# GpSimd prefills the bias buffers with the mask term and adds the bias by accumulating transfers

## The chip, the cores and the metric

The kernel runs on 1 core of one Trainium2 chip. The metric is the device time of one execution in microseconds, as the median of the runs.

## The reference

The model has four layers on 8 samples of 512 tokens with 256 features. The change touches the first, an attention block with 16 heads of 16 features, and the small inputs (token ids and angles) from which conditions are worked out. What matters of it:

```python
emb = silu(sin_emb(timestep)) @ W_ada + b_ada
scale, shift = split(emb[:, None, :], 2)
x = ln(src) * (1.0 + scale) + shift
q, k, v = heads(x @ Wq + bq), heads(x @ Wk + bk), heads(x @ Wv + bv)
scores = einsum('bhqd,bhkd->bhqk', q / sqrt(HEAD_DIM), k)
scores = scores + attention_bias          # (8, 16, 512, 512) float32, 134 MB
scores = where(src_mask, -inf, scores)    # (8, 1, 512, 512) bool
ctx = einsum('bhqk,bhkd->bhqd', softmax(scores), v)
x = x + (ctx @ Wo + bo)
# then a feed-forward layer, an adapter chosen by token, a rotation by angles, a second adapter
```

## The kernel before, in words

`attention_block` computes the first layer's attention, `network_block` behind it everything else, sample by sample. The change is in the first, in `setup_programs` (conditions), in `load_layouts`, and in the host part that lays out the small inputs.

Attention goes sample by sample: the first and the last are written out, the six between are a loop on each engine. A sample has STEPS = 64 steps, one for each head (16) and tile of 128 queries (4). Step n on TensorE (`iteration` in the tensor program): `scores` for step n + 3 (one bf16 matmul with 512 columns, L539, of stacked pieces of q and k, and one with the identity that adds the mask term, L540), four steps out of 16 `weigh` (values times turned probabilities, L562), `turn` (four 128x128 transposes of the probabilities, L549), and what `SPARE` places on two spare banks: transposes of x, projections Q, K, V of the next sample, context and output projection. VectorE adds the bias and takes the minimum of the negated row in one instruction (`add_bias`, L679, two steps ahead) and copies 3 of 8 turned tiles (L688); ScalarE takes the exponent (L820, one step ahead) and copies the other 5 of 8 (L827). So every engine has an order written out by hand, and semaphores with counts per sample stand between them.

The bias lies in `bias` (the buffer `big`): NB = 4 buffers of [128, 4, 512] float32, one per head. SP's program runs by heads: at head h of a sample it waits until VectorE has added the bias of all 4 tiles of head h (`biased`), then loads head h + 4 into the same buffer (`load_bias`, L415, 1 MB, its source rows of 2 KB). In the same queue, behind these waits, stand at fixed heads the loads of x, mask, the expert's weights, the stores of the pieces (`store_pieces`, L442, three transfers for q and three for k in each half of the heads), the loads of the stacks (`load_stack`, L453) and the store of x1.

The mask arrives as bytes in `mraw`. GpSimd makes from it the term (mask x -1e30, bf16) in two copies: `mterm_early` for heads 0 to 13 (L950, at step 56 for the next sample) and `mterm_late` for heads 14 and 15 (L958, at step 12), in four parts of 512 elements each. GpSimd also has, in this order within a sample: `copy_values` (L939, steps 5, 39, 41, 56), `keep_residual` (L967, step 15) and the four `cut`s (L925 to L929) at CUT_STEPS = 25, 26, 28, 31, in which the projections become three bf16 pieces. Cuts 2 and 3 wait until the stores of the pieces of cuts 0 and 1 have landed.

Ahead of the first sample `setup["load"]` issues ten loads on SP (token ids, angles four times, frequencies, pairs, W_ada, b_ada), then `first_loads` (x, identity, Wq, Wk, bq, bk, mask, Wv, bv, Wo, bo, and the bias of heads 0 to 3). VectorE waits for all ten before it works out the angles (L149 on), and four cuts of the first sample are made on VectorE, in the order of the banks, the value projection last.

## Time and profile before

| | us |
|---|---|
| median of 3 runs | 1149.35 |
| lowest and highest | 1147.81, 1149.48 |
| the profiled execution's own time | 1147.64 |
| its span, first to last instruction | 1145.8 |
| TensorE busy in the span | 1026.5 (90%) |
| VectorE busy | 818.1 (71%) |
| ScalarE busy | 776.6 (68%) |
| GpSimd busy | 349.4 (30%) |
| DMA, moved in all | 230.23 MB |

The page gives the busy time of each engine, the span in 40 slices of 28.6 us, the chain that ended last, the groups of instructions by line, and the transfers. PE is TensorE's matmul, PEld its weight load, DVE is VectorE, ACT ScalarE, POOL GpSimd, SP the engine that issues the transfers (SPq is its queue). L540 is line 540 of the kernel. Averages over the span hide that the first two thirds (attention) and the last third (network) have different limits; each stretch must be read by itself. "Idle before" names what a group waited for.

### The profile page before, as it was taken

What the parts mean: (1) busy time and instruction counts of PE and PEld (TensorE: products, weight loads), DVE (VectorE), ACT (ScalarE), POOL (GpSimd) and SP (SyncE); (2) the same over time, 40 slices, a digit from 0 to 9 for tenths busy, and PEclk for the clock granted to TensorE, in tenths of its full rate; (3) what the DMA queues carried; (4) which work ended last, traced back from release to release, by engine and by line L of the source; (5) the groups of instructions that cost most, each with busy time, mean ns of one, the idle gap of its engine ahead of it and who ended that gap; (6) DMA issues with size and microseconds to landing.
All of it is one profiled execution on the core that took longest, in us unless ns stands there. A gap on an engine that the chain in (4) does not pass through costs nothing. (4 is left out here: it accounts for less than half of the span.)

```text
span 1145.8 us, 21120 instructions
## 1 busy us (share of the span) xinstructions
PE 1026.5 (90%) x6128; PEld 670.0 (58%) x6128; DVE 818.1 (71%) x2056; ACT 776.6 (68%) x1238; POOL 349.4 (30%) x464
## 2 busy tenths in 40 slices
PE   2599999999999999999999999983999989898862
PEld 2456556656656565655655665642777767676641
DVE  5586775876787777778678686764456978897665
ACT  2287877887787788778788787863457565765442
POOL 0205114213312322320511511004455555654421
PEclk9799999999999999999999999996999999999976
DMA  7787976986995995896796797641111110101001
GB/s 237 241 299 262 353 274 232 367 294 225 338 326 191 340 349 204 305 356 233 275 362 245 250 371 266 247 151 37 38 37 38 37 55 18 55 18 37 19 19 37
DMA packets 131288, 230.23 MB, mean 201 GB/s; under 512 B 8992, under 2 KB 58016, under 8 KB 127136
## 3 DMA queue, kind: packets, MB, share of 16 engines
q1 hardware_dynamic: 131232, 229.59, 56.8%
q8 instruction: 22, 0.36, 0.1%
q14 instruction: 34, 0.28, 0.1%
HBM read 187.62 MB, written 41.94 MB: 200 GB/s over the span
## 5 line engine op out<-in xcount | busy, mean ns | idle before, releaser
L679 DVE CUSTOM_DVE_ANT_0 prob<-s_bank,big 128x512 f32<-128x512 f32 x512 | 344.8, 686 | 128.7 <-PE s_bank L540 103.0
L820 ACT ACTIVATE prob<-prob,nmax 128x512 f32<-128x512 f32 x512 | 359.6, 722 | 36.4 <-DVE nmax L679 35.2
L549 PEld LDWEIGHTS t_bank<-ident,prob 128*128 128x128 f32 x2048 | 241.0, 141 | 196.7 <-issue 71.2
L549 PE MATMUL t_bank<-ident,prob 128*128 128x128 f32 x2048 | 316.0, 277 | 8.0 <-DVE pt L688 4.7
L827 ACT COPY pt<-t_bank 128x512 f32<-128x512 f32 x320 | 185.1, 578 | 98.6 <-PE t_bank L549 98.0
L539 PE MATMUL s_bank<-stack_k,stack_q 128*128 128x512 bf16 x512 | 195.6, 382 | 4.6 <-DVE nmax L679 2.6
L540 PE MATMUL s_bank<-mterm_early,ident_bf 128*128 128x512 bf16 x448 | 170.8, 381 | 0.0
L688 DVE COPY pt<-t_bank 128x512 f32<-128x512 f32 x192 | 132.0, 687 | 48.9 <-PE t_bank L549 48.9
L562 PE MATMUL o_bank<-pt,val 128*32 128x512 f32 x1024 | 135.8, 604 | 0.7 <-ACT pt L827 0.7
L1624 POOL TENSOR_TENSOR gl<-big,gh 128x512 fp32r<-128x512 f32 x64 | 87.1, 1372 | 86.3 <-DVE gh L1329 86.3
L939 POOL TENSOR_SCALAR val<-vst 128x64 f32<-128x64 f32 x128 | 27.0, 245 | 251.8 <-PE o_bank L562 217.9
L1511 ACT ACTIVATE big<-bank,b 128x512 f32<-128x512 f32 x64 | 43.5, 689 | 42.8 <-PE bank L1191 41.9
L925 POOL TENSOR_SCALAR pieces<-proj 128x512 bf16<-128x512 f32 x28 | 17.4, 620 | 174.9 <-ACT proj L857 122.9
L539 PEld LDWEIGHTS s_bank<-stack_k,stack_q 128*128 128x128 bf16 x512 | 50.0, 98 | 26.6 <-issue 14.0
L1191 PE MATMUL bank<-hh,w1h 128*128 128x512 f32 x128 | 54.4, 425 | 11.6 <-ACT big L1511 6.7
L1210 PE MATMUL bank<-gh,w2h 128*128 128x512 f32 x128 | 54.0, 422 | 0.0
L562 PEld LDWEIGHTS o_bank<-pt,val 128*32 128x32 f32 x1024 | 20.4, 108 | 55.3 <-issue 51.8
L1191 PE MATMUL bank<-hh,w1l 128*128 128x512 f32 x128 | 51.7, 404 | 0.0
L1191 PE MATMUL bank<-hl,w1h 128*128 128x512 f32 x128 | 51.6, 403 | 0.0
L540 PEld LDWEIGHTS s_bank<-mterm_early,ident_bf 128*128 128x128 bf16 x448 | 44.2, 99 | 11.7 <-issue 7.8
L1210 PE MATMUL bank<-gh,w2l 128*128 128x512 f32 x128 | 50.9, 398 | 0.0
L1336 DVE TENSOR_TENSOR x24l<-x,x24h 128x512 fp32r<-128x512 f32 x32 | 47.9, 1536 | 1.0 <-ACT x24h L1519 0.5
(176 smaller groups left out, 1620.1 us busy)
## 6 DMA issues: line engine op xcount, KB each, us to landing
big<-in_fside_Bx16xSxS SPq DMA_DIRECT2D x128, 1024.0 KB, 6.6
pieces_dram<-pieces SPq DMA_DIRECT2D x64, 384.0 KB, 7.8
stack_q<-pieces_dram SPq DMA_DIRECT2D x16, 1024.0 KB, 8.0
stack_k<-pieces_dram SPq DMA_DIRECT2D x16, 1024.0 KB, 8.7
pieces_dram<-pieces SPq DMA_DIRECT2D x32, 256.0 KB, 7.5
xin<-in_x SPq DMA_DIRECT2D x8, 512.0 KB, 6.6
x_dram<-x SPq DMA_DIRECT2D x8, 512.0 KB, 2.6
big<-x_dram SPq DMA_DIRECT2D x8, 512.0 KB, 3.5
```

Source lines behind the costliest of these rows:

```text
L539: pe.matmul(bank, stack_q[:, h, t * P:(t + 1) * P], stack_k[:, h, :], start=True, stop=False)
L540: pe.matmul(bank, ident_bf[:], mterm[:, t, :], start=False, stop=True).then_inc(scored.sem, 1)
L549: last = pe.transpose(t_bank[n % 2][:, c * P:(c + 1) * P], prob[:, n % NT, c * P:(c + 1) * P], ident[:])
L562: last = pe.matmul(o_bank[VW * j:VW * (j + 1), :], val[:, c, G * g + j, :], pt[:, pt_slot(G * g + j), c, :], start=(c == 0), stop=(c == QT ...
L679: dve.tensor_tensor_reduce(out=prob[:, n % NT, :], in0=s_bank[n % 3][:, :], in1=bias[:, h % NB, t, :], scale=-1.0, scalar=3e38, op0=ALU.ad ...
L688: dve.tensor_copy(pt[:, pt_slot(h), :, t * P:(t + 1) * P], t_bank[n % 2][:, :].rearrange("p (c q) -> p c q", c=QT)).then_inc(evac[1].sem, 1)
L820: act.activation(tile, tile, ACT.Exp, bias=nmax[:, n % NT:n % NT + 1], scale=-1.0).then_inc(exped.sem, 1)
L827: act.copy(pt[:, pt_slot(h), :, t * P:(t + 1) * P], t_bank[n % 2][:, :].rearrange("p (c q) -> p c q", c=QT)).then_inc(evac[0].sem, 1)
L1191: last = pe.matmul(bank[f % 2][:, :], w[:, c, col], h[:, c, :], start=(n == 0), stop=(n == len(parts) - 1))
L1210: last = pe.matmul(bank[c][:, :], w[:, f, c * P:(c + 1) * P], gx[:, f, :], start=(m == 0), stop=(m == len(parts) - 1))
L1336: dve.tensor_tensor(x24l[:, l, c], src[:, c], x24h[:, l, c], ALU.subtract).then_inc(low_done[l].sem, 1)
L1624: pool.tensor_tensor(gl[:, f], g[:, f % NGT], gh[:, f], ALU.subtract).then_inc(gl_done.sem, 1)
```

## The change

The mask term is added no longer by TensorE. GpSimd writes it in float32 into a bias buffer as soon as that buffer is free, and then itself issues the load of the bias with accumulation (`accum_op=ADD`), so that the buffer ends up with bias plus mask term. TensorE's second matmul of each step, the bf16 identity and one of the two copies of the term go. The bias loads leave SP's program, with their waits. The mask term is made in one instruction of 2048 elements at step 49. GpSimd issues a load at the end of each head's last step (steps 3, 7, 11, ... in its order), between its cuts and value copies.

On the host, token ids are laid out in one array and angles, frequencies, pairs and the vectors b_ada, bq, bk, bo in another, so that two loads take the place of twelve; W_ada is loaded behind x. In the first sample the value projection is moved on VectorE between the cuts.

```diff
-    conds = [
-        (tok[:], d["itok_B_34_63"].partition_broadcast(P)), (dom[:], d["itok_B_0_15"].partition_broadcast(P)),
-        (arg[:, 2], d["condB_theta"].partition_broadcast(P)), (arg[:, 3], d["condB_theta"].partition_broadcast(P)),
-        (arg[:, 4], d["condB_phi"].partition_broadcast(P)), (arg[:, 5], d["condB_phi"].partition_broadcast(P)),
-        (freq[:], d["freq"]), (pairs[:], d["pairs"]), (w_ada, v["W_ada"]), (b_ada[:], v["b_ada"]),
-    ]
+        sp.dma_start(toks[:], d["toks"]).then_inc(vecs_in, 16)
+        sp.dma_start(vecs[:], d["vecs"]).then_inc(vecs_in, 16)
+
+    def load_weights(sp):
+        sp.dma_start(w_ada, v["W_ada"]).then_inc(w_ada_in, 16)
...
-EARLY_TERM_AT = QT * EARLY_HEADS
-LATE_TERM_AT = 12
+TERM_AT = 49
...
-        early = [(k["ident"][:], d["ident"]), (w["wq"], v["Wq"]), (w["wk"], v["Wk"]), (vec["bq"][:], v["bq"]),
-                 (vec["bk"][:], v["bk"])]
-        later = [(w["wv"], v["Wv"]), (bv[:], d["L0_cond_bv"].partition_broadcast(P)), (w["wo"], v["Wo"]),
-                 (vec["bo"][:], v["bo"])]
+        early = [(k["ident"][:], d["ident"]), (w["wq"], v["Wq"]), (w["wk"], v["Wk"])]
+        later = [(w["wv"], v["Wv"]), (bv[:], d["L0_cond_bv"].partition_broadcast(P)), (w["wo"], v["Wo"])]
...
-        first_loads += [(bias[:, h], v["bias"][:, h], bias_in[h]) for h in range(NB)]
...
-            for dst, src, arrived in first_loads:
+            for m, (dst, src, arrived) in enumerate(first_loads):
                 sp.dma_start(dst, src).then_inc(arrived, 16)
+                if m == 0:
+                    setup["load_weights"](sp)
...
-                    if not (last and h + NB >= H):
-
-                        sp.wait_ge(biased.sem, biased.at(b, QT * (h + 1)))
-                        apart(sp, sp_apart)
-                        load_bias(b, h + NB)
...
-                if n < QT:
-                    pe.wait_ge(early_term.sem, early_term.at(b - 1, n + 1))
-                if h == EARLY_HEADS:
-                    pe.wait_ge(late_term.sem, late_term.at(b, t + 1))
 
                 before = n - 3 if n >= 3 else (63, 61, 62)[n] - STEPS
                 pe.wait_ge(biased.sem, biased.at(b, before + 1))
                 bank = s_bank[n % 3][:, :]
-                mterm = mterm_early if h < EARLY_HEADS else mterm_late
-                pe.matmul(bank, stack_q[:, h, t * P:(t + 1) * P], stack_k[:, h, :], start=True, stop=False)
-                pe.matmul(bank, ident_bf[:], mterm[:, t, :], start=False, stop=True).then_inc(scored.sem, 1)
+                pe.matmul(bank, stack_q[:, h, t * P:(t + 1) * P], stack_k[:, h, :], start=True, stop=True
+                          ).then_inc(scored.sem, 1)
...
+            at = {use[:2]: m for m, use in enumerate(banks.uses)}
+            spare_use(banks, at["XT", 0], -1, first=True)
+            spare_use(banks, at["XT", 1], -1, first=True)
+            low_parts(-1)
+            dve.wait_ge(weights_in, 16 * len(later))
+            dve.wait_ge(w_high, 3)
+            dve.tensor_tensor(wl["wv"][:], w["wv"], wh["wv"][:], ALU.subtract).then_inc(w_low, 1)
+            cut(0)
+            cut(1)
+            spare_use(banks, at["V", 0], -1, first=True)
+            cut(2)
+            spare_use(banks, at["V", 1], -1, first=True)
+            cut(3)
...
-            def early_mask_term(b, t, first=False):
-                if t == 0:
-                    pool.wait_ge(mask_in.sem, mask_in.at(b, 16))
+            def mask_term(b):
+                pool.wait_ge(mask_in.sem, mask_in.at(b, 16))
+                apart(pool, pool_apart)
+                pool.tensor_scalar(mterm[:], mraw[:], MASKED, 0.0, ALU.mult, ALU.add).then_inc(term_done.sem, 1)
+
+            def load_bias(b, h, first=False):
+
+                if h % H == 0:
+                    pool.wait_ge(term_done.sem, term_done.at(b, 1))
                 if not first:
-                    pool.wait_ge(scored.sem, scored.at(b, QT * (EARLY_HEADS - 1) + t + 1))
+                    pool.wait_ge(biased.sem, biased.at(b, QT * (h - NB + 1)))
                 apart(pool, pool_apart)
-                pool.tensor_scalar(
-                    mterm_early[:, t, :], mraw[:, t, :], MASKED, 0.0, ALU.mult, ALU.add
-                ).then_inc(early_term.sem, 1)
-
-            def late_mask_term(b, t, first=False):
-                if t == 0 and not first:
-                    pool.wait_ge(scored.sem, scored.at(b - 1, STEPS))
+                pool.tensor_scalar(bias[:, h % NB], mterm[:], 1.0, 0.0, ALU.mult, ALU.add
+                                   ).then_inc(prefilled.sem, 1)
+                pool.wait_ge(prefilled.sem, h + 1 if first else prefilled.at(b, h - NB + 1))
                 apart(pool, pool_apart)
-                pool.tensor_scalar(
-                    mterm_late[:, t, :], mraw[:, t, :], MASKED, 0.0, ALU.mult, ALU.add
-                ).then_inc(late_term.sem, 1)
+                src = v["bias"][:, h] if first else v["bias"][:, bass.ds(b * H + h, 1)].rearrange(
+                    "p o t k -> p (o t) k")
+                pool.dma_start(bias[:, h % NB], src, accum_op=ALU.add).then_inc(bias_in[h % NB], 16)
 
             def keep_residual(b, first=False):
...
-                    if n == LATE_TERM_AT:
-                        for t in range(QT):
-                            late_mask_term(b, t, first=first)
-                    if not last and n == EARLY_TERM_AT:
-                        for t in range(QT):
-                            early_mask_term(b, t)
-
-            for t in range(QT):
-                early_mask_term(-1, t, first=True)
+                    if n % QT == QT - 1 and not (last and n // QT + NB >= H):
+                        load_bias(b, n // QT + NB)
+                    if not last and n == TERM_AT:
+                        mask_term(b)
+
+            mask_term(-1)
+            for h in range(NB):
+                load_bias(-1, h, first=True)
```

## Rows read from the trace of the kernel before

**Rows 1.** The page, the span in 40 slices: granted TensorE clock and DMA share, in tenths.
```profile
PEclk9799999999999999999999999996999999999976
DMA  7787976986995995896796797641111110101001
```

**Rows 2.** Table by stretches: stretch, length, busy us, clock, DMA share, GB/s.
```profile
50.00:762.00 712.00, 700.93 (x4664) 420.05 (x4664) 529.64 (x1432) 561.59 (x932) 172.44 (x308) 1.00 0.80 285
430.00:520.00 90.00, 88.86 (x598) 53.66 (x597) 66.71 (x179) 70.68 (x118) 23.66 (x41) 1.00 0.83 292
```

**Rows 3.** Groups by line, 430 to 520 us: busy, mean ns, idle before.
```profile
L679 DVE CUSTOM_DVE_ANT_0 prob<-s_bank,big 128x512 f32<-128x512 f32 x64 | 43.1, 685 | 16.5 <-PE s_bank L540 13.2 <-issue 3.1
L827 ACT COPY pt<-t_bank 128x512 f32<-128x512 f32 x40 | 23.1, 579 | 12.5 <-PE t_bank L549 12.4
```

**Rows 4.** Timeline of TensorE from 444 us: start, length, engine, line, operation.
```profile
444.52 0.38 PE L539 MATMUL s_bank<-stack_k,stack_q 128*128 128x512 bf16 x1
444.74 0.38 PE L540 MATMUL s_bank<-mterm_early,ident_bf 128*128 128x512 bf16 x1
445.05 1.06 PE L562 MATMUL o_bank<-pt,val 128*32 128x512 f32 x8
```

**Rows 5.** The page's issues of transfers: KB each, median us from issue to landing.
```profile
big<-in_fside_Bx16xSxS SPq DMA_DIRECT2D x128, 1024.0 KB, 6.6
pieces_dram<-pieces SPq DMA_DIRECT2D x64, 384.0 KB, 7.8
stack_q<-pieces_dram SPq DMA_DIRECT2D x16, 1024.0 KB, 8.0
```

**Rows 6.** Table by stretches, three short ones with the DMA engines full.
```profile
448.60:451.40 2.80, 2.80 (x18) 2.11 (x17) 2.05 (x7) 2.56 (x5) 0.00 (x0) 1.00 1.05 386
312.00:314.00 2.00, 2.00 (x17) 1.66 (x16) 1.96 (x8) 1.72 (x4) 1.81 (x3) 1.00 1.06 406
478.00:486.00 8.00, 8.00 (x61) 5.51 (x59) 7.73 (x24) 7.97 (x15) 0.00 (x0) 1.00 0.99 369
```

**Rows 7.** Line 415: issue ns min, median, max, first and last start; us to landing.
```profile
L415 SPq DMA_DIRECT2D big<-in_fside_Bx16xSxS x124: 367/373/1167, 55.5 to 745.6; - x124
...
DMA to landing us min/median/max: 5.0/6.5/14.4
```

**Rows 8.** Groups of GpSimd by line, whole span.
```profile
L950 POOL TENSOR_SCALAR mterm_early<-mraw 128x512 bf16<-128x512 uint8 x32 | 19.9, 621 | 17.9 <-DMA mraw<-in_mask_Bx1xSxS_bk 15.5
...
L967 POOL TENSOR_SCALAR xres<-xt 128x1024 f32<-128x1024 f32 x8 | 8.4, 1048 | 77.2 <-issue 77.2
```

**Rows 9.** Timeline of GpSimd around the cuts: first and last pieces of cuts.
```profile
452.59 0.62 POOL L925 TENSOR_SCALAR pieces<-proj 128x512 bf16<-128x512 f32 x1 [15.51 <-ACT proj L857]
...
455.36 1.17 POOL L929 TENSOR_TENSOR pieces<-rest,pieces 128x512 bf16<-128x512 f32 x1
...
459.58 1.17 POOL L929 TENSOR_TENSOR pieces<-rest,pieces 128x512 bf16<-128x512 f32 x1
...
467.25 0.62 POOL L925 TENSOR_SCALAR pieces<-proj 128x512 bf16<-128x512 f32 x1 [6.51 <-DMA pieces_dram<-pieces]
...
474.24 1.16 POOL L929 TENSOR_TENSOR pieces<-rest,pieces 128x512 bf16<-128x512 f32 x1
```

**Rows 10.** Timeline of SP in the same stretch.
```profile
459.35 4.90 SPq L442 DMA_DIRECT2D pieces_dram<-pieces  x6
```

**Rows 11.** Timeline of the start: SP, VectorE, TensorE.
```profile
0.73 0.40 SPq L130 DMA_DIRECT2D tok<-in_itok_B  x1
...
4.96 0.47 SPq L130 DMA_DIRECT2D b_ada<-in_L_cond_b_ada  x1
...
11.62 0.17 DVE L149 CAST tokf<-tok 128x8 f32<-128x8 int32 x1 [7.93 <-DMA b_ada<-in_L_cond_b_ada]
...
51.32 0.38 PE L539 MATMUL s_bank<-stack_k,stack_q 128*128 128x512 bf16 x1 [1.87 <-DVE vst L731]
```

**Rows 12.** Issues of transfers, two of the conditions: KB, us to landing.
```profile
tok<-in_itok_B SPq DMA_DIRECT2D x1, 4.0 KB, 2.2
...
b_ada<-in_L_cond_b_ada SPq DMA_DIRECT2D x1, 2.0 KB, 6.6
```

More of the change, by code:

```diff
@@ L90, in load_layouts @@
         v[w] = d["L0_cond_" + w].rearrange("(c p) n -> p c n", p=P)
-    for w in BY_FEATURE:
+    for w in BY_FEATURE[len(VECTORS):]:
         v[w] = d["L0_cond_" + w]
@@ L158, in angles @@
         link(dve.tensor_scalar(arg[:, 1], tokf[:, 1], freq[:, 0:1], None, ALU.mult))
-        link(dve.scalar_tensor_tensor(turns[:], arg[:], 1.0 / (2.0 * np.pi), quarter[:], ALU.mult, ALU.add))
+        link(dve.scalar_tensor_tensor(turns[:], arg, 1.0 / (2.0 * np.pi), quarter[:], ALU.mult, ALU.add))
         link(dve.tensor_scalar(turns[:], turns[:], 12582912.0, None, ALU.add))
@@ L164, in angles @@
         for part in TWO_PI_PARTS:
-            link(dve.scalar_tensor_tensor(arg[:], turns[:], -part, arg[:], ALU.mult, ALU.add))
-        link(dve.scalar_tensor_tensor(arg[:], quarter[:], 2.0 * np.pi, arg[:], ALU.mult, ALU.add))
-        dve.tensor_scalar(arg[:], arg[:], 3.1415925, -3.1415925, ALU.min, ALU.max).then_inc(sines, 1)
+            link(dve.scalar_tensor_tensor(arg, turns[:], -part, arg, ALU.mult, ALU.add))
+        link(dve.scalar_tensor_tensor(arg, quarter[:], 2.0 * np.pi, arg, ALU.mult, ALU.add))
+        dve.tensor_scalar(arg, arg, 3.1415925, -3.1415925, ALU.min, ALU.max).then_inc(sines, 1)
     def domains(dve):
-        link(dve.tensor_copy(k["domf"][:, 0], dom[:]))
+        link(dve.tensor_copy(k["domf"][:, 0], dom))
         link(dve.tensor_scalar(k["domf"][:, 1], k["domf"][:, 0], 0.0, E - 1.0, ALU.max, ALU.min))
@@ L193, in sines_of @@
         act.wait_ge(sines, 1)
[L194 removed]
+        act.activation(k["trig"][:], arg, ACT.Sin).then_inc(sines, 1)
         act.wait_ge(sines, 2)
@@ L793, in _ @@
                 dve.tensor_tensor(wl[name][:], w[name], wh[name][:], ALU.subtract).then_inc(w_low, 1)
[L794 to L806 removed]
+            dve.tensor_scalar(bq_scaled[:], vec["bq"], HD ** -0.5, None, ALU.mult).then_inc(bq_made, 1)
+            at = {use[:2]: m for m, use in enumerate(banks.uses)}
[11 more added lines that the diff above has]
+            cut(3)
             for n in range(2):
@@ L1751 @@
     place = np.arange(P) % 4
-    arrays["pairs"] = np.stack([place < 2, place >= 2], 1).astype(np.float32)
+    pairs = np.stack([place < 2, place >= 2], 1).astype(np.float32)
     beside = np.zeros((P, P), np.float32)
```

67 lines of the change are left out of this document (26 added, 41 removed).

## The prediction, made before the change was run

> **What bounds the kernel now.** I read the page's slices first. The kernel has two parts: attention over 8 samples, up to about 762 us, and the network behind it, which the change doesn't touch. In the first part TensorE is granted its full clock and the DMA share stands at 7 to 9 tenths; in the second the DMA share is one tenth [rows 1]. So only the first part can gain or lose much, and there two resources are near their end.
>
> The table by stretches gives both numbers. From 50 to 762 us TensorE is busy for 701 of 712 us at clock 1.00, ACT 562, DVE 530, GpSimd 172, and the DMA engines 0.80 of the time, which is 570 us. One sample in the middle (430 to 520) is the same: TensorE 88.9 of 90, DMA 0.83 [rows 2]. TensorE is the bound: DVE's bias line sits idle before PE's mask matmul, ACT's copy before PE's transposes [rows 3]. A sample takes 712 / 8 = 89 us, a step (one head, one tile of 128 queries, 64 steps per sample) 89.4 / 64 = 1.40 us. The second resource is what this change leans on: DMA has 142 us left in 712, and no more.
>
> **What the change takes from TensorE.** In the timeline of one step the score matmul starts at 444.52, the mask matmul at 444.74 and the next work at 445.05 [rows 4]. Starts 0.22 us apart are what a 512-column bf16 matmul takes of the pipeline; the 380 ns printed overlap. 512 such matmuls go: 512 x 0.22 = 113 us, all on the path that sets the end, if nothing else is late. The floor of the first part is then 712 - 113 = 599 us. ACT (562) and DVE (530) stay below that, with little room: they are the next two bounds.
>
> **What the bias transfers cost.** Per sample 16 bias loads of 1 MB, 12 stores of pieces and 4 stack loads [rows 5]. Short stretches at full share move 386 GB/s (448.6 to 451.4, a bias load alone at first) and 406 (312 to 314) [rows 6], so I take 400: 1.05 MB / 400 GB/s = 2.62 us of all 16 engines. The 124 loads issued in this part [rows 7] cost 124 x 2.62 = 325 of the 570 us; everything else 245. After the change each bias transfer must read the source, read what GpSimd wrote in SBUF, and write. No row of before shows such a transfer. The bounds: 1.0 times the plain load if the second read runs wholly beside the write, 2.0 times if the engine takes its reads one after another and they set its pace, as would a load and a store of the same 1 MB in a row. A count of passes (three for two) says 1.5. HBM is not what separates them, since it carries the same bytes. I take the middle between the count of passes and the count of reads, 1.75, because a stretch with loads and stores mixed (478 to 486) is already at share 0.99 with 369 GB/s [rows 6]: the engines, by their time per byte, are at their end, and there is no idle side into which a second read would fall. Demand: 570 + 0.75 x 325 = 814 us. At a share of 0.98 (the longest of these full stretches shows 0.99) that takes 831 us against 712 now: +119 us. With 1.5 it is (570 + 163) / 0.98 = 748, +36 us; with 2.0, 913, +201 us; with 1.0, 582, which is under TensorE's 599.
>
> The Trainium skill bears on this (Collectives: The Full Stack, "Part 3: Why 7x under link rate"): reduce-scatter runs at about half of all-gather's rate, 32.35 against 62.28 GB/s, since the add needs two reads on the same ring. By that ratio, 1.93, the first part would be at (570 + 0.93 x 325) / 0.98 = 890 us, +178; no run here shows an accumulating transfer yet. It speaks against the change, and it is the rival of the two reads below.
>
> **What GpSimd gets.** Its tensor_scalar takes 0.62 us for 512 elements and 1.05 us for 1024 [rows 8]: 0.84 ns per element and 0.19 us fixed, so 2048 elements take 1.9 us, if a bf16 source goes as the f32 and uint8 ones do; the ends are 1.7 (no fixed part) and 2.5 us (four times 0.62). Per sample: busy now 23.7; the two mask terms (8 x 0.62 = 5.0) become one of 1.9; 16 prefills add 30.4: 51 us. To this come 16 issues of a transfer. GpSimd issues none now; SP's take 0.37 us at the median and 1.17 at most [rows 7]. A queue that an engine has to fill itself may take longer than either; I take 1 us, with 0.4 and 3.5 as ends (the upper end an estimate: one issue per 1 MB at three times SP's slowest). 51 + 16 = 67 of 89 us: no bound by itself, and it becomes one at (89.4 - 51) / 16 = 2.4 us per issue.
>
> But GpSimd works in order. Queued ahead of a bias load are the four cuts of a sample and their waits. Cuts 0 and 1 run from 452.6 to 460.8, cut 2 waits until 467.25 for the store of the pieces, cut 3 ends at 475.4 [rows 9]. In the new order the load for head 10 (step 27) stands between cuts 1 and 2 and fits in that wait; the load for head 11 (step 31) stands behind cut 3. It would be issued at 475.4 + 1.9 + 1 = 478.3 and land 6.5 us later [rows 7], at 484.8. VectorE wants head 11 at its step 42, 17 steps after cut 0: 452.6 + 17 x 1.40 = 476.4. That is 8.4 us late. SP no longer waits for bias buffers ahead of the stores, which were issued at 459.35 though the first cut was done at 456.5 [rows 9, 10]: this gives 2.8 back. So 6 us of stall per sample (bounds 3 and 9), in the 7 samples that prepare the next: +42 us. Behind this wait stand all scores, so TensorE and ACT too. Before, the same load sat on SP, which nothing but the buffer held up. In a DMA-bound run this stall is also a time in which few bias loads are queued, so it adds up with the 119.
>
> **The start.** VectorE's first step on the conditions begins at 11.62, after the last of ten small loads, which was issued at 4.96; the first was issued at 0.73 [rows 11]. Two packed loads are issued by 1.6 and land 2.2 to 6.6 us later, as the small loads do [rows 12], so this start moves up by 3.4 to 7.8 us, take 6. The value projection now stands in the waits of the cuts; it is the last work ahead of the first scores at 51.32 [rows 11], but these also need the first stack loads, so 1 us. The loads of the first four heads start later and go through GpSimd; they have until the first scores and are done by about 33 us even at 3 us per issue. Sum -7 (bounds -10 and -2). The mask load, now released by one mask term, costs nothing: it is wanted some 50 steps after its issue.
>
> **Sum.** The profiled run of before has a span of 1145.8 and a time of 1147.6 us; the median of the runs is 1149.35, 1.7 above. 1147.6 - 7 + 119 + 42 = 1301.6, and 1.7 for the median: 1303 us. TensorE's 113 us vanish: its steps are 0.22 us shorter, and it waits for bias.
>
> **The rivals.**
> - Other side: the second read is free (factor 1.0). TensorE stays the bound at 599 us, DMA at 582 just under it: 1149.35 - 7 - 113 + 42 = 1071 us. For it: the read side of an engine may have room in a plain load, which the profile can't show since it prints one busy share for both sides. Against: the full stretches. Its place is the transfer from HBM to the bias buffer, its price 2.6 us. It decides as follows: with the stall of 42 and the start of -7 the first part may take 712 - 35 = 677 us, which is a demand of 663 = 570 + 93, so the factor must be below 1 + 93 / 325 = 1.29 for the kernel to be faster.
> - The two reads set the pace in full (factor 2.0): 1149.35 - 7 + 201 + 42 = 1385 us. For it: a load and a store of the same size in a row would cost that. Against: reads come from two memories, and the write of a plain load may be what fills its time.
> - GpSimd is the bound: if an issue takes 3 us, GpSimd has 51 + 48 = 99 us per sample and the 6.5 us that it waits for the store, 105.5. 8 x (105.5 - 89.4) = +129 us, 1149.35 - 7 + 129 = 1271 us. For it: it writes 2048 elements and describes 512 rows for each head. Against: only that it idles two thirds of its time now.
> - Nothing is gained or lost: factor near 1.29, 1149 us.
> - A part not doing what it says: if TensorE's time were not shortened since ACT is next, the fast case would lose up to 562 / 0.98 = 573 < 599, so nothing; I drop it.
>
> **Chances.** DMA-bound forecast 0.34, two reads in full 0.13, GpSimd-bound 0.17, fast 0.32, no change 0.04. The slower cases fall inside the range with the bounds of their costs: 1.5 with a stall of 3 per sample gives 1149 - 7 + 36 + 21 = 1199; 2.0 with 9 gives 1149 - 7 + 201 + 63 = 1406. The fast case begins at 1149 - 10 - 113 + 21 = 1047 if all goes well and sits at 1071. The likeliest case's own range is 1199 to 1370; the range for 8 in 10 reaches down to the fast case and up to two reads, 1065 to 1410. Faster by over 0.2% (about what a measurement of this kernel can tell from no change) 0.32, within 0.04, slower 0.64.
>
> **What would show it.** In the profile after: the DMA share in the first part at 9 to 10 tenths with less than 300 GB/s counted by bytes written, or, if it is GpSimd, its share near 9 tenths with DMA below 8. VectorE's bias line idle before the landing of bias transfers and not before TensorE. The time from issue to landing of a bias transfer at 9 us or more, against 6.6. Head 11 of each sample late by some us while GpSimd is in its cuts. VectorE's first step on conditions at 4 to 8 us. TensorE's busy share well below 0.9 and perhaps a clock below 1.00 as it waits. I am wrong if bias transfers land in 7 us or less with TensorE still busy for over 97% of a shorter first part.

## The result, and the profile after

The changed kernel takes 1276.16 us (median of 4 runs, 1275.11 to 1278.75) against 1148.58 for the kernel before beside it: 1.1117 times as long, 95% interval 1.1101 to 1.1134, or +128 us. The forecast was 1303, range 1065 to 1410, slower.

The profiled run of after has a span of 1273.1 us and a time of 1275.1. Its page, beside [rows 1]: the granted clock of TensorE and the share of the DMA engines in 40 slices, then the two queues (packets, MB, share of 16 engines), and the bias transfers (KB each, median us from issue to landing), which answer to [rows 5].

```profile
PEclk9798999789799989979988897899889999999966
DMA  7999999999999999999999999999201010100000
...
q0 software_dynamic: 67584, 134.23, 57.8%
q1 hardware_dynamic: 62208, 95.37, 21.9%
...
big<-in_fside_Bx16xSxS POOLq DMA_DIRECT2D x128, 1024.0 KB, 14.9
```

After the first slice (the start), every slice of the first part is at nine tenths or more, where before showed 5 to 9. In finer stretches of 10 us, from 60 to 880 us, after reads a share of 1.02 to 1.20; before is under 1.0 in 49 of its 69. The bias transfers stand in a queue of their own now (q0), and land 14.9 us after their issue at the median, 6.6 before. TensorE's granted clock is no longer full throughout.

The table by stretches (stretch, length, busy us of PE, PEld, DVE, ACT and POOL with counts, clock, DMA share, GB/s) answers to [rows 2]. The scores run in after from 53 to 891 us. In the 4 us of the second row nearly all that moves are accumulating transfers; in the 5 us of the third there are plain transfers beside them. They answer to [rows 6].

```profile
53.00:891.00 838.00, 670.92 (x4164) 396.27 (x4163) 524.88 (x1434) 562.40 (x935) 541.95 (x486) 0.91 1.11 243
526.00:530.00 4.00, 4.00 (x27) 3.12 (x26) 3.03 (x8) 3.85 (x8) 3.34 (x5) 1.00 1.12 206
530.00:535.00 5.00, 5.00 (x38) 3.35 (x37) 3.77 (x12) 3.84 (x7) 3.93 (x4) 1.00 1.09 336
```

The first part is 838 us long, 712 before: +126 of the +128. TensorE is busy for 671 of them, GpSimd for 542, and no engine is near its end but the DMA engines: share 1.11, at 243 GB/s where before had 285. The short stretch of accumulating transfers has 206 GB/s, half of the 386 and 406 of plain loads in [rows 6]: 1.049 MB / 206 GB/s = 5.1 us for a head's bias, 2.6 to 2.7 before. The 14.9 us from issue to landing hold waiting as well: one is issued every 838 / 124 = 6.8 us, so two or three are under way at a time, beside the plain ones.

Two groups of the page show who waits (busy, mean ns, idle before and its releaser); they answer to [rows 3] and [rows 8]. The two groups of issues behind them are of after and of the experiment e1 below, in which the same transfers are plain (issue ns min/median/max, first and last start).

```profile
L655 DVE CUSTOM_DVE_ANT_0 prob<-s_bank,big 128x512 f32<-128x512 f32 x512 | 339.1, 686 | 272.2 <-DMA big<-in_fside_Bx16xSxS 207.1
...
L933 POOL TENSOR_SCALAR big<-mterm 128x2048 f32<-128x2048 bf16 x128 | 259.2, 2025 | 76.1 <-DVE nmax L655 70.5
```

```profile
L939 POOL DMA_DIRECT2D big<-in_fside_Bx16xSxS x128: 1300/1307/1461, 15.6 to 874.7; - x128
...
DMA to landing us min/median/max: 8.9/14.9/22.4
```

```profile
L939 POOL DMA_DIRECT2D big<-in_fside_Bx16xSxS x128: 797/797/944, 14.6 to 759.0; - x128
...
DMA to landing us min/median/max: 5.5/6.0/12.5
```

VectorE's bias line stood 207 us before the landing of a bias transfer, where before it stood behind TensorE. GpSimd's write takes 2.0 us and its issue 1.3, 0.8 when the transfer doesn't accumulate.

The network behind attention is unchanged: from the last bias step to the end of the run lie 383.8 us (1275.1 - 891.3), before 383.6 (1147.6 - 764.0).

### The profile page after: what moved, and what is told of

Its sections match the earlier page's. It is cut to its first block and busy times, and to the rows that moved or that the text cites. A ratio compares the mean times of both kernels' runs of the same rounds, so it can differ in the third digit from the quotient of the medians.

```text
span 1273.1 us, 20268 instructions
## 1 busy us (share of the span) xinstructions
PE 993.3 (78%) x5616; PEld 642.1 (50%) x5616; DVE 822.4 (65%) x2055; ACT 775.7 (61%) x1238; POOL 737.2 (58%) x664
## 3 DMA queue, kind: packets, MB, share of 16 engines
q0 software_dynamic: 67584, 134.23, 57.8%
q1 hardware_dynamic: 62208, 95.37, 21.9%
## 5 line engine op out<-in xcount | busy, mean ns | idle before, releaser
L655 DVE CUSTOM_DVE_ANT_0 prob<-s_bank,big 128x512 f32<-128x512 f32 x512 | 339.1, 686 | 272.2 <-DMA big<-in_fside_Bx16xSxS 207.1
L526 PE MATMUL t_bank<-ident,prob 128*128 128x128 f32 x2048 | 352.2, 299 | 118.6 <-DVE pt L664 79.1
L526 PEld LDWEIGHTS t_bank<-ident,prob 128*128 128x128 f32 x2048 | 257.3, 152 | 316.8 <-DVE pt L664 111.7
L933 POOL TENSOR_SCALAR big<-mterm 128x2048 f32<-128x2048 bf16 x128 | 259.2, 2025 | 76.1 <-DVE nmax L655 70.5
L516 PE MATMUL s_bank<-stack_k,stack_q 128*128 128x512 bf16 x512 | 211.9, 415 | 61.3 <-DVE nmax L655 49.0
L939 POOL DMA_DIRECT2D big<-in_fside_Bx16xSxS x128 | 167.6, 1310 | 91.3 <-POOL big L933 85.6
L539 PE MATMUL o_bank<-pt,val 128*32 128x512 f32 x1024 | 142.5, 632 | 0.7 <-ACT pt L804 0.7
L516 PEld LDWEIGHTS s_bank<-stack_k,stack_q 128*128 128x128 bf16 x512 | 53.1, 104 | 90.6 <-DVE nmax L655 65.8
L916 POOL TENSOR_SCALAR val<-vst 128x64 f32<-128x64 f32 x128 | 39.4, 596 | 72.6 <-PE o_bank L539 54.8
L1372 DVE TENSOR_SCALAR xh<-bank,mv,rstd 128x256 f32<-128x256 f32 x96 | 45.6, 537 | 1.2
## 6 DMA issues: line engine op xcount, KB each, us to landing
big<-in_fside_Bx16xSxS POOLq DMA_DIRECT2D x128, 1024.0 KB, 14.9
```

The costliest lines, as they stand in the source:

```text
L516: pe.matmul(bank, stack_q[:, h, t * P:(t + 1) * P], stack_k[:, h, :], start=True, stop=True).then_inc(scored.sem, 1)
L526: last = pe.transpose(t_bank[n % 2][:, c * P:(c + 1) * P], prob[:, n % NT, c * P:(c + 1) * P], ident[:])
L539: last = pe.matmul(o_bank[VW * j:VW * (j + 1), :], val[:, c, G * g + j, :], pt[:, pt_slot(G * g + j), c, :], start=(c == 0), stop=(c == QT ...
L655: dve.tensor_tensor_reduce(out=prob[:, n % NT, :], in0=s_bank[n % 3][:, :], in1=bias[:, h % NB, t, :], scale=-1.0, scalar=3e38, op0=ALU.ad ...
L933: pool.tensor_scalar(bias[:, h % NB], mterm[:], 1.0, 0.0, ALU.mult, ALU.add).then_inc(prefilled.sem, 1)
L939: pool.dma_start(bias[:, h % NB], src, accum_op=ALU.add).then_inc(bias_in[h % NB], 16)
```

## The experiments

Twelve changed kernels follow. The kernel before took 1148.3 to 1148.6 us beside them. Some leave part of the mask out of the scores, as their texts say: they are there for their times.

| kernel | us | ratio (95%) |
|---|---|---|
| before | 1148.58 | |
| after | 1276.16 | 1.1117 (1.1101 to 1.1134) |
| e1 plain, GpSimd writes and issues | 1160.75 | 1.0105 (1.0088 to 1.0122) |
| e2 plain, SP issues, no write | 1084.89 | 0.9445 (0.9430 to 0.9461) |
| e3 the packed conditions alone | 1140.08 | 0.9921 (0.9904 to 0.9937) |
| e4 after, with a matmul of zeros per step | 1289.28 | 1.1211 (1.1182 to 1.1239) |
| e5 e1 with cuts 2 and 3 later | 1161.36 | 1.0121 (1.0104 to 1.0138) |
| e6 after with cuts 2 and 3 later | 1285.60 | 1.1192 (1.1171 to 1.1212) |
| e7 e3, accumulation for heads 4, 7, 9, 13 | 1183.45 | 1.0310 (1.0292 to 1.0327) |
| e9 e3, GpSimd adds in the buffer, 8 heads | 1138.51 | 0.9912 (0.9896 to 0.9929) |
| e10 e1 without GpSimd's write | 1148.97 | 1.0002 (0.9992 to 1.0011) |
| e11 after, accumulation in odd heads only | 1192.05 | 1.0381 (1.0363 to 1.0398) |
| e12 as e9, 6 heads | 1125.51 | 0.9805 (0.9788 to 0.9821) |
| e13 as e7, heads 4, 6, 8 | 1127.84 | 0.9825 (0.9809 to 0.9842) |

The theory: accumulating transfers fill the DMA engines and set the pace; behind it the loads that stand behind GpSimd's cuts. The rivals: GpSimd's work or its order alone does it, or TensorE's lower clock.

**e1, no accumulation.**

```
-                pool.dma_start(bias[:, h % NB], src, accum_op=ALU.add).then_inc(bias_in[h % NB], 16)
+                pool.dma_start(bias[:, h % NB], src).then_inc(bias_in[h % NB], 16)
```

> The changed kernel with the accumulation taken out of the transfer: GpSimd still writes the mask term into each buffer, still waits for it and still issues the load, but the load overwrites it. So the mask is left out of the scores. Theory A (the accumulating transfer takes the DMA engines twice as long, 5.1 us against 2.6 for 1 MB, and this sets the pace): the time falls from 1276 to 1040 to 1080 us, below the kernel before, and TensorE is busy for over 90% of the attention part. Theory B (GpSimd's 2 us of writing, 1.3 us of issuing and its order set the pace): it stays above 1200 us. Between 1040 and 1080 lies the stall behind the cuts that the prediction put at 42 us.

It takes 1160.75, between the ranges of the two theories, so neither forecast was met. Accumulation costs 1276.2 - 1160.8 = 115 us, and everything else together +12. So GpSimd as the bound falls as an account of the 128. But the rest isn't the gain that the prediction's fast case had: with each transfer at its plain price this kernel is still slower than before.

**e2, no work on GpSimd either.** The write is gone, and SP issues plain loads as before, behind its own waits; TensorE adds no mask.

```
+                    if not (last and h + NB >= H):
+                        sp.wait_ge(biased.sem, biased.at(b, QT * (h + 1)))
+                        load_bias(b, h + NB)
...
-                    if n % QT == QT - 1 and not (last and n // QT + NB >= H):
-                        load_bias(b, n // QT + NB)
```

> As e1_plain_pool, but GpSimd writes nothing into the buffers and SP issues the plain loads at the places they had before; the mask is left out of the scores. This is what taking the mask's matmul from TensorE is worth with nothing put in its place. Both theories: 1030 to 1045 us (1149 less 512 x 0.22 = 113, and some us of start). The difference to e1_plain_pool is what GpSimd's part costs by itself: 42 us by the prediction's stall behind the cuts, 5 or less if the four buffers cover it.

It takes 1084.89, some 40 us more than expected: TensorE's matmuls were worth less than 113 us. How much less, e3 tells.

**e3, the packed conditions alone**, on the kernel before: the two packed tensors, the late load of W_ada, the value projection between the cuts.

```
+        sp.dma_start(toks[:], d["toks"]).then_inc(vecs_in, 16)
+        sp.dma_start(vecs[:], d["vecs"]).then_inc(vecs_in, 16)
...
-        dve.wait_ge(cond_in, 16 * len(conds))
+        dve.wait_ge(vecs_in, 32)
```

> The kernel before with the packed conditions, the later W_ada and the value projection between the cuts, and nothing else of the change. If the start of the changed kernel is late since GpSimd's writes hold up VectorE there (its 128x2 operation took 2.78 us instead of 0.16), this kernel has its first scores 6 to 10 us earlier than before and takes 1139 to 1143 us. If the packing itself is worth nothing, since transfers of the pieces set the first scores, it stays within 2 us of 1149.

e3 takes 1140.08, 8 us less than before. From e3 to e2 the mask's matmuls go, with their waits, and GpSimd makes one mask term of 1.9 us in place of two (5.0 us a sample): 1140.1 - 1084.9 = 55 us, half of the 113 that the prediction took off TensorE's path. The same stretch of both, e3 first:

```profile
60.00:690.00 630.00, 618.52 (x4074) 374.26 (x4151) 465.88 (x1253) 494.62 (x820) 164.69 (x286) 1.00 0.82 287
```

```profile
60.00:690.00 630.00, 593.02 (x3959) 348.18 (x4033) 499.06 (x1362) 530.56 (x895) 144.36 (x238) 1.00 0.87 311
```

The groups of VectorE's bias line in these stretches count the steps:

```profile
L677 DVE CUSTOM_DVE_ANT_0 prob<-s_bank,big 128x512 f32<-128x512 f32 x442 | 298.2, 686 | 116.2 <-PE s_bank L538 94.3 <-issue 20.6
```

```profile
L668 DVE CUSTOM_DVE_ANT_0 prob<-s_bank,big 128x512 f32<-128x512 f32 x486 | 321.5, 685 | 79.6 <-PE s_bank L529 46.4 <-remote 20.4 <-issue 11.5
```

A step is 630 / 442 = 1.425 us in e3 and 630 / 486 = 1.296 in e2. TensorE's busy time per step goes from 618.5 / 442 = 1.399 to 593.0 / 486 = 1.220, 0.18 less, near the 0.22 of the prediction; its idle time grows from 0.026 to 0.076. Of 0.22 us a step, 0.13 arrived: over 512 steps 66 us, of which the run shows 55. In the busiest stretches the next engines are full, as in this one of e2, where VectorE is busy for 14.73 of 15 us and ACT for 14.29:

```profile
385.00:400.00 15.00, 13.62 (x78) 7.80 (x77) 14.73 (x45) 14.29 (x24) 1.05 (x1) 1.00 0.84 320
```

That these take the idle 0.05 fits, but what each idle piece waits for was not separated.

**e10, GpSimd issues but doesn't write.** e1 without these lines:

```
-                pool.tensor_scalar(bias[:, h % NB], mterm[:], 1.0, 0.0, ALU.mult, ALU.add
-                                   ).then_inc(prefilled.sem, 1)
-                pool.wait_ge(prefilled.sem, h + 1 if first else prefilled.at(b, h - NB + 1))
```

> e1_plain_pool without GpSimd's write into the buffer and the wait for it: GpSimd only issues the plain loads, in the same order among its cuts and copies; the mask is left out of the scores. e5 showed that moving two cuts is worth nothing, so the 76 us between e2 (1085) and e1 (1161) are open. If they come from what GpSimd has to do per head (1.9 us of writing and 0.7 of waiting, which make its loads late after each pile-up), this kernel is at 1085 to 1100 us. If they come from GpSimd issuing (its queue, the order behind the cuts), it stays at 1140 to 1160.

It takes 1148.97, 64 us more than e2, from which it differs in who issues the loads and in what order. The queue itself isn't slow: its loads land 7.9 us after their issue at the median, 7.4 in e2. Its timeline of GpSimd, and VectorE's step behind it (start, length, engine, line, operation, idle before and its releaser), answer to [rows 9]:

```profile
459.96 0.80 POOL L935 DMA_DIRECT2D big<-in_fside_Bx16xSxS  x1 [0.82 <-POOL pieces L906]
...
468.13 0.62 POOL L902 TENSOR_SCALAR pieces<-proj 128x512 bf16<-128x512 f32 x1 [3.40 <-DMA pieces_dram<-pieces]
...
470.89 1.17 POOL L906 TENSOR_TENSOR pieces<-rest,pieces 128x512 bf16<-128x512 f32 x1
472.89 1.55 POOL L935 DMA_DIRECT2D big<-in_fside_Bx16xSxS  x2 [0.83 <-POOL pieces L906]
```

```profile
482.13 0.69 DVE L655 CUSTOM_DVE_ANT_0 prob<-s_bank,big 128x512 f32<-128x512 f32 x1 [8.39 <-DMA big<-in_fside_Bx16xSxS]
```

This is the stall that the prediction worked out: head 10's load fits ahead of cut 2, head 11's is issued when cut 3 is done, and VectorE stands for 8.4 us. The waits of VectorE from 200 to 700 us (total us, times, longest) say how often, in e10 and, below it, in e1:

```profile
DVE prob L655 <- DMA big<-in_fside_Bx16xSxS: 51.5, 6, 9.5
```

```profile
DVE prob L655 <- DMA big<-in_fside_Bx16xSxS: 52.4, 12, 6.7
```

Six waits of 8.6 us on average in six samples. Over the whole of e10 there are seven, of 8.0 to 9.5 us, together 60 of the 64 us; in e2 VectorE has no such wait in this stretch. The write on top (e10 to e1) costs 12 more, but not in this wait: it is split into two of together the same size, and 8 of the 12 come at the start, where the first scores move from 40.95 to 48.91 us.

**e5 and e6, cuts 2 and 3 behind the load of head 11**, in e1 and in after:

```
-                    if not last and n in CUT_STEPS:
+                    if not last and n in CUT_STEPS[:2]:
                         cut(b, CUT_STEPS.index(n))
...
                         load_bias(b, n // QT + NB)
+                    if not last and n == CUT_STEPS[3]:
+                        cut(b, 2)
+                        cut(b, 3)
```

> e1_plain_pool (plain loads issued by GpSimd, mask left out of the scores) with cuts 2 and 3 moved behind the load of head 11, and nothing else. If the 76 us between e1 and e2 are mostly the wait for head 11 behind the cuts (VectorE waited 64 us for bias transfers in e1, up to 6.7 us at a time), 50 to 60 of them come back: 1100 to 1112 us against 1160.75. If they are GpSimd's own time (prefill 1.9, wait 0.7, issue 0.8 us per head) or its holding up of VectorE, the time moves by less than 10 us.

> The changed kernel with the same move of cuts 2 and 3. If the stall behind the cuts adds up with the DMA engines' time, as the prediction had it, the kernel gains what e5 gains, 50 us or so: 1225. If the DMA engines are the one bound and have plain transfers to work on meanwhile, it stays within 10 us of 1276.

e5 takes 1161.36, the same as e1 within the intervals: a miss for the stall as I had put it. Its timeline shows why. Head 12's load now stands behind all the cuts:

```profile
474.45 0.80 POOL L939 DMA_DIRECT2D big<-in_fside_Bx16xSxS  x1 [0.73 <-POOL big L933]
...
486.35 0.80 POOL L939 DMA_DIRECT2D big<-in_fside_Bx16xSxS  x1 [0.73 <-POOL big L933]
...
494.57 0.69 DVE L655 CUSTOM_DVE_ANT_0 prob<-s_bank,big 128x512 f32<-128x512 f32 x1 [5.14 <-DMA big<-in_fside_Bx16xSxS]
```

The pile of work was moved, not taken away: VectorE's waits for bias transfers, 64.0 us in all of e1, are still 51.6 in e5, and its waits for TensorE's scores rise from 49.7 to 78.6. What makes the scores late there was not separated. Whether the move helps without the write (e10 with the cuts later) was not tried. e6 takes 1285.60, 9 us more than after: in the accumulating kernel the move of the cuts is worth nothing, or less. But since the move gained nothing in e5 either, e6 can't tell whether the stall adds up with the DMA engines' time; the profile of after can (below).

**e4, TensorE's work back.** After, with a second bf16 matmul of 512 columns, of zeros, in each step:

```
+                pe.matmul(bank, zero_w[:], zero_m[:], start=False, stop=True).then_inc(scored.sem, 1)
```

> The changed kernel with a bf16 matmul of zeros added in each step where the mask's matmul was, so TensorE's work is that of before. Theory A (the DMA engines set the pace): the time stays within 1% of 1276 us, though 113 us of TensorE's work are back. If part of TensorE's waiting is its own, or the lower granted clock (0.91) costs something, it moves: up by as much as 113 us if the work adds up, or down if a busier TensorE keeps its clock.

It takes 1289.28 (interval of the ratio to before 1.1182 to 1.1239), a hair over the 1% named. TensorE's busy time in the first part rises from 671 to 744 us, by the prediction's count its pipeline has 113 us more work, and 13 us of it arrive at the end. So TensorE doesn't set the pace. Nor does its lower clock: 0.91 in the first part of after, 0.94 in e4, which is slower. In e4 the DMA engines aren't full throughout any more (7 of 82 stretches of 10 us read under 1.0, none in after); that the 13 us lie there is likely, but was not taken apart.

**e11 and e13, fewer accumulating transfers.** e11 is after with accumulation in odd heads only. e13 is e3 with the whole change for heads 4, 6 and 8 of each sample (written, issued and accumulated by GpSimd, no mask by TensorE), all others as before.

```
-                pool.dma_start(bias[:, h % NB], src, accum_op=ALU.add).then_inc(bias_in[h % NB], 16)
+                pool.dma_start(bias[:, h % NB], src, **(dict(accum_op=ALU.add) if h % 2 else {})).then_inc(bias_in[h % NB], 16)
```

```
+BY_POOL = (4, 6, 8)
...
-                    if not (last and h + NB >= H):
+                    if not (last and h + NB >= H) and h + NB not in BY_POOL:
...
+                    if n % QT == QT - 1 and n // QT + NB in BY_POOL:
+                        load_bias(b, n // QT + NB)
```

> The changed kernel with the accumulation in the loads of the 8 odd heads alone; the even heads' loads overwrite, so their mask is left out. GpSimd's work is the same. With 62 accumulating transfers of 5.1 us in place of 2.6 in the loop the DMA engines' demand is about 730 us. If the engines' time decides by a threshold (free until they are full), the time lies near e1's 1161, at 1165 to 1190. If each accumulating transfer costs its 2.5 us or more whatever the load, it lies half way, at 1215 to 1225.

> As e7_accum_4_heads but for heads 4, 6 and 8 alone, whose transfers are issued ahead of the cuts and the stores of pieces. In e7 one head per sample (13, issued behind the cuts, 13.9 us to landing beside the stores) kept VectorE waiting 9.5 us, which over 7 samples makes more than the 43 us lost. If the place was the trouble, this one is at 1130 to 1142 us. If accumulating transfers cost by themselves, 24 x 2.5 = 60 us of the engines' time, it is above 1150.

e11 takes 1192.05, 2 us above the range of the threshold and far from the other. The first 62 of the 124 accumulating transfers cost 1192.1 - 1160.8 = 31 us, the second 62 cost 84: no fixed price each, but a reserve that is used up. It isn't used up at one point: e11's mean share is 0.99, yet 48 of its 74 stretches of 10 us are at 1.0 or more, and there the transfers queue. e13 takes 1127.84, 12 us less than e3: with 3 of 16 heads' matmuls gone, 3/16 of the 55 us are 10, so its 24 accumulating transfers cost nothing that can be told. The rows of the first part, of e3, e13, e11, e1, e6 and e4 in this order:

```profile
42.00:755.00 713.00, 698.69 (x4588) 422.27 (x4671) 531.18 (x1434) 563.48 (x935) 166.63 (x289) 0.99 0.81 285
```

```profile
42.00:744.00 702.00, 684.03 (x4496) 412.36 (x4579) 530.08 (x1436) 561.88 (x936) 244.70 (x339) 0.99 0.92 290
```

```profile
50.00:807.00 757.00, 637.51 (x4085) 385.44 (x4161) 526.75 (x1434) 559.72 (x934) 511.20 (x486) 0.93 0.99 269
```

```profile
49.00:773.00 724.00, 634.91 (x4086) 381.90 (x4162) 525.94 (x1434) 557.99 (x934) 477.67 (x486) 0.95 0.80 281
```

```profile
53.00:899.00 846.00, 681.75 (x4163) 398.40 (x4161) 525.80 (x1434) 563.03 (x935) 543.01 (x486) 0.89 1.10 240
```

```profile
53.00:907.00 854.00, 744.45 (x4592) 440.04 (x4675) 530.98 (x1436) 570.56 (x936) 543.18 (x486) 0.94 1.09 238
```

Share times length is the work of the DMA engines. It is 578 us in e3 (0.81 x 713) and 579 in e1, both with no accumulating transfer. With 24 of them (e13) it is 646, with 62 (e11) 749, with 124 (after, e6, e4) 930, 931 and 931. The surplus per transfer is 68 / 24 = 2.8, 170 / 62 = 2.7 and 352 / 124 = 2.8 us: the same in every kernel. A plain load is worth 2.72 us x 1.05 = 2.85 on this scale (386 GB/s at share 1.05 in [rows 6]), so the factor is 2.0, and the stretch of accumulating transfers says so too: 5.09 us x 1.12 = 5.7. After, e6 and e4 have one and the same work, in lengths of 838, 846 and 854 us, at a share of 1.11 to 1.09. That the engines end near 1.11 with this mix is read from after itself, where no stretch of 10 us is under 1.02.

A rival for the factor is the packets: the page of e1 has fewer of them in GpSimd's queue than that of after. e1 (q0, 128 bias loads), and e3 (q1, the same loads by SP and all other transfers, which are 62208 packets in after):

```profile
q0 software_dynamic: 34816, 134.23, 32.6%
```

```profile
q1 hardware_dynamic: 129792, 229.60, 57.5%
```

A plain load has 272 packets in e1 and (129792 - 62208) / 128 = 528 in e3, as many as an accumulating one (67584 / 128). Yet e1 and e3 have the same work, 579 and 578 us. So neither the number of packets nor GpSimd's queue makes the factor of two; the accumulation does.

**e7, which heads.** As e13 with four heads, one of which (13) is issued behind cuts and copies.

```
-BY_POOL = (4, 6, 8)
+BY_POOL = (4, 7, 9, 13)
```

> e3_packed_only with the change made for 4 of 16 heads alone (4, 7, 9, 13): GpSimd writes the term and adds the bias by an accumulating transfer, TensorE adds the mask for the other 12. If an accumulating transfer costs 2.5 us of the DMA engines more than a plain one, 32 x 2.5 = 79 us of demand are added to 570, which still fits under 712 - 28 us: 1113 to 1140 us, at or below e3 (1140). If the DMA engines' spare 17% can't be used up (bursts), it is above 1140.

1183.45, where e13 takes 1127.84: one head more and two at other places cost 56 us. Head 13's transfer is issued at 397.14 and lands 13.9 us later, and VectorE stands for it, in this sample and in six others:

```profile
397.14 1.32 POOL L980 DMA_DIRECT2D big<-in_fside_Bx16xSxS  x1 [0.96 <-POOL big L975]
```

```profile
411.08 0.69 DVE L685 CUSTOM_DVE_ANT_0 prob<-s_bank,big 128x512 f32<-128x512 f32 x1 [9.45 <-DMA big<-in_fside_Bx16xSxS]
```

The seven waits are 9.4 to 10.2 us, 67 us together, which more than covers the 56. What a transfer costs depends on where it stands in the order of an engine as much as on its price.

**e9 and e12, the add in SBUF.** On e3: SP loads every bias plain, and for some heads GpSimd adds the mask term in the buffer, four tensor_tensor of 512 elements; TensorE adds the mask for the others. e9 has heads 2 to 7, 13 and 14, e12 has 2, 3 and 12 to 15, whose adds meet neither VectorE's normalising of x nor its making of the low parts.

```
+                for t in range(QT):
+                    pool.tensor_tensor(bias[:, h % NB, t], bias[:, h % NB, t], term[:, t], ALU.add
+                                       ).then_inc(masked.sem, 1)
```

> e3_packed_only with, for 8 of 16 heads (2 to 7, 13, 14), plain bias loads by SP and the mask term added in the buffer by GpSimd (four tensor_tensor of 512 elements per head, 1.2 us each), TensorE adding the mask for the other 8 alone. The DMA engines have nothing more to do. e2 gained 55 us on e3 with all 16 matmuls gone, so with half of them this one should gain 20 to 28: 1112 to 1120 us. If GpSimd's 4 to 5 us per head come late or hold up VectorE, it gains nothing: 1140 or more.

> As e9_add_in_place but for the 6 heads 2, 3, 12, 13, 14, 15, whose adds on GpSimd fall in no step in which VectorE normalises x or makes its low parts. In e9 those VectorE operations took 0.92 and 1.63 us instead of 0.41 and 0.69. If that was what ate e9's gain, this one takes 6/16 of the 55 us that e2 gained: 1118 to 1125 us. If GpSimd's adds hold up more than that, or TensorE's saved time isn't on the path in these steps, it is within 5 us of e3's 1140.

e9 takes 1138.51, hardly less than e3's 1140.08: 64 x 4 mask matmuls fewer brought nothing that can be told. e12 with 48 x 4 fewer takes 1125.51, the fastest complete version run, 0.9805 times before; e13 (1127.84) is next. The adds take 1.16 to 1.18 us each on GpSimd, 4.7 per head. In e9 two of VectorE's groups are held up beside them (busy, mean ns; 409 and 689 ns in e3, 408 and 688 in e12):

```profile
L709 DVE TENSOR_SCALAR xin<-xin,mv,rstd 128x256 f32<-128x256 f32 x28 | 25.6, 973 | 0.3
...
L717 DVE TENSOR_TENSOR xtl<-xt,xth 128x512 fp32r<-128x512 f32 x14 | 20.4, 1498 | 0.9
```

## Why the prediction was right, and where it wasn't

The parts of the 128 us as the runs give them, one change at a time: packed conditions -8 (e3), the mask's matmuls -55 (e3 to e2), loads in GpSimd's order +64 (e2 to e10), GpSimd's write and its wait +12 (e10 to e1), accumulation +115 (e1 to after). They are the steps of this one order; in another, a part could count for more or less, since a wait that is there alone can vanish behind another.

**The bound before, and the second resource.** Right. TensorE was the bound and the DMA engines had two tenths of the time left; after, that is used up. That relieving TensorE alone gives 55 us (e3 to e2) shows the one, the work of 578 us before and 930 after the other. (One small slip in its numbers: 712 / 8 is 89.0 us a sample, and the 89.4 used behind it is in no row; it moves the GpSimd rival by 3 us and hardly anything else.)

**The price of a transfer (1.75) and the ceiling (0.98).** Both were off, and they offset each other, so that 831 stands beside a measured 838 is luck. On the scale of the share a plain load is 2.85 us, not 2.62, and the factor is 2.0, not 1.75; it was the count of reads, the upper bound, that held. The accumulation adds 352 us of work, where the forecast had 0.75 x 325 = 244. And the share ends at 1.11, not at 0.98: I had taken the highest mixed stretch of before for the end of the engines, though [rows 6] also showed 1.05 and 1.06. With all of it corrected: (578 + 124 x 2.85) / 1.11 = 839 us. That is no test of the 1.11, which comes from the same run; the price of 2.85 is borne out by e11 and e13. The rival with factor 2.0 had the right factor and said 1385: with the ceiling at 1.11 its first part is (570 + 325) / 1.11 = 806, so it was too high by the 0.98 and would then be too low by the 2.62. By bytes alone the factor is 400 / 206 = 1.94. The Trainium skill's ratio (Collectives: The Full Stack, "Part 3: Why 7x under link rate") was 1.93: this case's trace agrees with it. The estimate worked out from it, +178, had the same two faults: with the ceiling at 1.11 it is (570 + 0.93 x 325) / 1.11 = 786 us, +74, where +126 were measured. That the reason is a second read, as that page has it, no run here shows.

**The stall behind the cuts (+42).** The mechanism was right and its size near. The waits in e10 are 8.0 to 9.5 us per sample, not 6. Its timeline gives the terms: cut 3 ends 21.1 us after the start of cut 0 (472.06 - 451.00) instead of 22.8, so SP's earlier stores gave back 1.8 and not 2.8 (cut 2 didn't wait at all, cut 3 for 3.4 us); the load landed 9.2 us after its issue (482.1 - 472.9) and not 6.5, with head 12's load issued right behind it; and VectorE wants head 11 after 17 steps of 1.30 us, not 1.40, which is 1.7 us earlier. The 0.8 us between cut and issue stands for the 2.9 of the sum, since e10 writes no mask. Together 21.1 + 0.8 + 9.2 - 22.1 = 9.0, where the timeline has 8.4. The step that failed is "it adds up with the 119". In after the stall is there: the load of head 11 of one sample, issued behind cut 3, and VectorE's step that needs it; then the stretch in which VectorE stands.

```profile
439.55 1.31 POOL L939 DMA_DIRECT2D big<-in_fside_Bx16xSxS  x1 [1.10 <-issue]
```

```profile
451.95 0.69 DVE L655 CUSTOM_DVE_ANT_0 prob<-s_bank,big 128x512 f32<-128x512 f32 x1 [7.08 <-DMA big<-in_fside_Bx16xSxS]
```

```profile
444.90:451.90 7.00, 3.75 (x15) 2.65 (x13) 0.00 (x0) 1.20 (x3) 6.28 (x11) 0.50 1.11 230
```

VectorE stands for 7.1 us, and in this time the share is 1.11, the mean of the first part: transfers already issued fill the DMA engines. Their work of 930 us at that share is the 838 us of the first part, with nothing left for a stall on top. Where the full resource works through a stall, the two don't add up. How long the accumulating kernel would take with its loads in a better order was not run; the full share leaves it little to gain.

**TensorE's 113 us.** In the forecast they vanished, so the sum didn't need them, but the fast rival did. Its own condition, a transfer at the plain price, is e1: it gave 1071, and e1 takes 1160.75. The 113 were 55, the 42 were 64, the start -7 was about 0, and the write costs a little. So there is no break-even factor of 1.29: even at the plain price this kernel is 1% slower than before, and the chance of 0.32 was too high.

**GpSimd.** The prices were right: 1.9 us per write (1.887 to 1.897, and 2.4 right behind an issue), 1.3 us per issue against 1 assumed, 542 of 838 us busy. It was no bound by its busy time. As a rival it was wrong for the 128, though its order is worth 64 us while the DMA engines have room.

**The start (-7).** The packing did what was said: VectorE's conditions begin at 3.9 us instead of 11.62, and e3's first scores at 40.80 instead of 51.32. But in after they come at 52.6, one later than before. e1 stands at 48.91 and e10 at 40.95, so GpSimd's first writes cost 8 us and the accumulation another 4. The prediction had looked only at when the first bias is needed, not at what the writes do to VectorE beside them (below).

**Sum.** Forecast: start -7, first part 831 + 42 = 873. Measured: start +1, first part 838. 8 us too low and 35 too high make the 27 by which 1303 missed 1276. What was to be seen in the profile was there: the share at its end with 243 GB/s, VectorE before the landing of the bias, 14.9 us to land, TensorE below 0.9 busy and at a clock of 0.91.

## What to carry to other kernels

Ask of a transfer what it costs the DMA engines, not only whether it saves an instruction: an accumulating one costs them twice a plain one here, and this kernel, which used eight tenths of them, had room for a few (24 of 124, well placed), not for all. Give an engine that works in order only those loads that don't stand behind its long work and its waits, and don't trust a move until you have looked at which load is behind the work now. Measure the gain of the part that looks sure as well: with the bound engine relieved, half of the time that was taken off it arrived at the end.

## What the runs showed of the hardware that I had not expected

**VectorE's operations wait for GpSimd's.** At the start of after, operations of VectorE take much longer than in e3. The timeline of VectorE in after, then GpSimd's in the same time, then VectorE's in e3:

```profile
15.50 4.35 DVE L680 TENSOR_SCALAR xin<-xin,mv,rstd 128x256 f32<-128x256 f32 x4
...
20.80 2.63 DVE L769 TENSOR_TENSOR wql<-con,wqh 128x512 fp32r<-128x512 f32 x1
23.36 0.68 DVE L769 TENSOR_TENSOR wkl<-con,wkh 128x512 fp32r<-128x512 f32 x1
23.96 2.78 DVE L770 TENSOR_SCALAR bq_scaled<-vecs 128x2 f32<-128x2 f32 x1
```

```profile
20.46 2.42 POOL L933 TENSOR_SCALAR big<-mterm 128x2048 f32<-128x2048 bf16 x1
23.47 1.30 POOL L939 DMA_DIRECT2D big<-in_fside_Bx16xSxS  x1 [0.58 <-POOL big L933]
24.29 2.43 POOL L933 TENSOR_SCALAR big<-mterm 128x2048 f32<-128x2048 bf16 x1
```

```profile
13.44 1.38 DVE L702 TENSOR_SCALAR xin<-xin,mv,rstd 128x256 f32<-128x256 f32 x4
...
15.77 0.69 DVE L791 TENSOR_TENSOR wql<-con,wqh 128x512 fp32r<-128x512 f32 x1
...
16.98 0.16 DVE L792 TENSOR_SCALAR bq_scaled<-vecs 128x2 f32<-128x2 f32 x1
```

An operation on two elements per partition goes from 0.16 to 2.78 us and ends at 26.74, when GpSimd's write of 24.29 to 26.72 ends; the subtraction that meets no write keeps its 0.68. The Trainium skill (SBUF — State Buffer, "SBUF: two separate sides") says that one pair of ports is an exclusive lock between a GpSimd operation and certain of VectorE's, for the whole instruction; the trace agrees, by these ends. The short operation is recorded from 23.96 on, 0.3 us ahead of the write and beside GpSimd's issue of 23.47, so which of these two held it first isn't shown. From 60 to 880 us of after the same groups aren't slower (408 and 689 ns), and in e9 they are: it depends on what meets what.

**The work of both kinds of transfer adds up.** A stretch of accumulating transfers moves 206 GB/s, one with plain stores and loads beside them 336 (530 to 535, above). By the share, 124 x 5.7 = 707 of the 930 us are the accumulating ones, which leaves 223 for all others, and these were 578 - 124 x 2.85 = 225 in e3: side by side they cost what they cost apart.

**An accumulating transfer takes longer to issue.** 1.31 us on GpSimd against 0.80 for the same shape plain.

**The DMA share isn't bounded by one.** Full stretches read 0.99 to 1.06 in before and 1.12 in after (up to 1.20 over 10 us), so the highest share seen is a poor ceiling for another mix.
